# An expert stage written out for 64 experts, with thirteen weight places, narrower slot rows, and the last-slot weights transposed at the end

## The reference, cut to what matters

```
scores = softmax(h @ gate_weight.T)            # 2048 tokens x 64 experts
# 3 of 8 groups by their maximum, then the 6 best experts: topk_w, topk_i
pos  = running count of the expert over all (token, k)
slot = topk_i * 96 + minimum(pos, 95)          # later ones overwrite the last slot
buf  = zeros.at[slot].set(h[token])            # 64 x 96 x 256
out  = (silu(buf @ Wg.T) * (buf @ Wu.T)) @ Wd.T    # per expert, M = 176
y    = sum_k out[slot] * topk_w
shared = (silu(h @ Sg.T) * (h @ Su.T)) @ Sd.T  # 352 wide
x + gb * (y + shared)
```

## Time and profile before

| | |
|---|---|
| median of 3 runs | 1085.55 us (1081.42 to 1085.63) |
| profiled execution | 1088.81 us, its span 1087.0 us, mean granted clock 0.98 |
| busy: PE, DVE, ACT, POOL | 92%, 55%, 52%, 37% of the span |
| attention | to about 790 us |
| shared expert, last routing | about 790 to 857 us |
| expert stage, first to last scatter | 864.9 to 1053.6 us |
| the end | to 1087.0 us |

### The profile page before, as it was taken

One profiled execution on the slowest core, in us unless ns is written; L12 is line 12 of the kernel. 1 busy time (PEld: TensorE's weight loads), 2 busy tenths in 40 slices (PEclk: granted clock), 3 DMA queues, 4 the chain that ended last, 5 costly groups with the idle time before them and its releaser, 6 DMA issues.

```text
span 1087.0 us, 17987 instructions
## 1 busy us (share of the span) xinstructions
PE 1005.2 (92%) x6045; PEld 877.3 (81%) x6045; DVE 600.1 (55%) x1419; ACT 565.9 (52%) x1041; POOL 405.6 (37%) x598
## 2 busy tenths in 40 slices
PE   4999999999999999999999999999999888788883
PEld 4899999999999999999999999999755545444452
DVE  3555556666568656666865766685476311111117
ACT  2666666666766666676665666666430233233320
POOL 3122222233224554322455422255507244444450
PEclk9899999999999999999999999999999999999985
DMA  9990000001000110100011012000040499999946
GB/s 351 340 351 13 0 0 1 1 1 39 1 2 25 50 50 25 39 2 2 25 49 37 15 40 85 2 11 23 3 140 4 118 250 249 239 252 259 248 77 220
DMA packets 60138, 98.85 MB, mean 91 GB/s; under 512 B 8127, under 2 KB 41674, under 8 KB 59560
## 3 DMA queue, kind: packets, MB, share of 16 engines
q1 hardware_dynamic: 41992, 76.90, 21.6%
q0 software_dynamic: 11808, 14.16, 6.5%
q10 hardware_dynamic: 6272, 6.93, 2.4%
HBM read 65.31 MB, written 40.68 MB: 98 GB/s over the span
## 4 chain that ended last, share of the span: by engine, by line
PE 68%; DMA 14%; DVE 10%; issue 4%; ACT 2%; POOL 1%; POOLq 0%; SPq 0%; ACTq 0%; DVEq 0%
PE ps L1216 23%; DMA acc<-wos,arena 12%; PE ps L1266 12%; PE ps L1242 11%; PE ps L1255 9%; PE ps L1225 2%; PE ps L1228 2%; PE ps L1303 2%; PE ps L1249 2%; PE ps L1372 1%; PE ps L1426 1%; DMA arena<-slot_rows 1%; DVE ss L819 1%; DVE bst L746 1%; DMA warena<-in_wqkv 1%
## 5 line engine op out<-in xcount | busy, mean ns | idle before, releaser
L421 POOL TENSOR_TENSOR holdp<-neghalf 128x1 f32<-128x1 f32 x145 | 31.1, 215 | 477.2 <-ACT prob L583 242.0
L577 ACT ACTIVATE prob<-ps,rn 128x512 f32<-128x512 f32 (+3 forms) x256 | 121.0, 526 | 137.1 <-PE ps L1242 129.4
L1216 PE MATMUL ps<-wh,hth 128*128 128x384 f32 x512 | 178.2, 348 | 5.4 <-DVE htl L772 3.2
L1216 PE MATMUL ps<-wh,htl 128*128 128x384 f32 x512 | 172.9, 338 | 0.0
L1216 PE MATMUL ps<-wl,hth 128*128 128x384 f32 x512 | 172.7, 337 | 0.0
L819 DVE TENSOR_REDUCE ss<-arena 128x8 f32<-128x1024 f32 x64 | 78.1, 1220 | 150.6 <-ACT arena L553 150.5
L1266 PEld LDWEIGHTS ps<-vx,prob 128*128 128x128 f32 x1280 | 152.9, 191 | 3.9 <-POOL prob L468 0.7
L1266 PE MATMUL ps<-vx,prob 128*128 128x129 f32 (+1 forms) x1280 | 153.4, 274 | 0.4 <-POOL prob L468 0.4
L553 ACT ACTIVATE arena<-ps 128x1024 f32<-128x1024 f32 x64 | 65.5, 1023 | 141.3 <-PE ps L1216 141.3
L532 POOL DMA_INDIRECT acc<-wos,arena x64 | 90.2, 1409 | 116.8 <-DMA acc<-wos,arena 80.3
L1255 PE MATMUL ps<-wos,arena 128*128 128x256 f32 (+1 forms) x512 | 121.0, 379 | 0.8 <-ACT arena L587 0.8
(11 more groups left out here) (177 smaller groups left out, 1876.8 us busy)
## 6 DMA issues: line engine op xcount, KB each, us to landing
wge<-in_wgu SPq DMA_DIRECT2D x32, 352.0 KB, 4.5
slot_rows<-pay SPq DMA_DIRECT2D x1, 7728.0 KB, 37.4
arena<-slot_rows ACTq DMA_DIRECT2D x56, 120.8 KB, 4.1
wde<-in_wd SPq DMA_DIRECT2D x32, 192.0 KB, 4.2
prob<-in_wgu SPq DMA_DIRECT2D x16, 352.0 KB, 4.6
arena<-in_wgu SPq DMA_DIRECT2D x16, 352.0 KB, 4.2
warena<-in_wqkv SPq DMA_DIRECT2D x1, 4992.0 KB, 20.8
acc<-zrow SPq DMA_DIRECT2D x2, 2048.0 KB, 29.9
```

Of the source, the lines that this page charges most:

```text
L577: act_(prob[:, OFF[j]:OFF[j] + w], sflat[:, OFF[j]:OFF[j] + w], ACT.Tanh, scale=rn[:, bass.ds(head(n), 1), TT + j:TT + j + 1].squeeze(1)). ...
L1216: last = mm(ps[:, i, 0:3 * DH], hp[:, k, i * P:(i + 1) * P], wp[:, k, :], start=(k == 0 and m == 0), stop=(k == KC - 1 and m == 2))
```

## The change

It does these things:

- The ring of weights has 13 places. Seven gate/up places (GEARLY) and four down places are filled at the program's start, the other six and nine in the burst behind attention. Two accumulators stay.
- PE, ACT, DVE and SP have all 64 experts written out, with constants for addresses and waits.
- A slot row has 269 words: h, six weights, six expert numbers, the token. `route_probs` and its wait are gone; DVE multiplies the six best values by the inverse sum. For each expert DVE picks the weight with one compare-multiply-sum into `wcol`, and ACT takes its scale from there.
- The modulation's rows: `rcur` holds three rows of the current batch and is loaded anew for each batch by SP, `rgb` the gate row of all four.
- The transposes of w95 and their copies (now ACT's) come behind the last expert; w95's weights are formed with one more DVE operation per batch.
- At the end DVE multiplies the last rows by the gate rows of the batches (`o95g`), PE multiplies by that, and DVE adds PE's product to x as soon as it is there (`last_added`), and the accumulators' sum, scaled, later (`sums_added`).

```
-RING = 8
+GEARLY = 7
+RING = 13
-RW = 322
-TOK = D + E
+TOK = D + 2 * K
+RW = TOK + 1
...
-        rows = sb("rows", [P, B, 4, D])
+        rcur = sb("rcur", [P, 3, D])
+        rgb = sb("rgb", [P, B, D])
...
+            for u in range(GEARLY):
+                sp.dma_start(wgus[u], wgu[u]).then_inc(w_in[u], 16)
             for u in range(EARLY):
-                sp.dma_start(wgus[u], wgu[u]).then_inc(w_in[u], 16)
                 sp.dma_start(wds[u], wd[u]).then_inc(w_in[u], 16)
...
+            def rows_of(b):
+                sp.dma_start(rcur[:].rearrange("p c d -> p (c d)"),
+                             mod_d[b, 0:3, :].rearrange("c d -> (c d)").unsqueeze(0).to_broadcast([P, 3 * D])).then_inc(s["rows_in"], 16)
...
                 sp.dma_start(h2_rows[:, bass.ds(b, 1)].squeeze(1), pay[:, :, 0:D]).then_inc(s["h2_out"], 16)
+                rows_of(b + 1)
...
             for u in range(EARLY, RING):
-                sp.dma_start(wgus[u], wgu[u]).then_inc(w_in[u], 16)
+                if u >= GEARLY:
+                    sp.dma_start(wgus[u], wgu[u]).then_inc(w_in[u], 16)
                 sp.dma_start(wds[u], wd[u]).then_inc(w_in[u], 16)
...
+            for e in range(E + 2):
+                if e + RING < E:
+                    gate_up(e)
+                if e >= 2:
+                    if e - 2 + RING < E:
+                        down(e - 2)
+                    last_row(e - 2)
...
-            def route_probs(b):
-
-                a.wait_ge(s["sum_inv"], b + 1)
-                for i in range(TT):
-                    ins = act_(pay[:, i, D:TOK], lg[:, i, :], ACT.Copy, scale=rs[:, i:i + 1])
-                ins.then_inc(s["probs"], 1)
...
+                a.wait_ge(s["wcol_rdy"], base + e + 1)
                 act_(orow[:, e % ORING, :], ps[0:C, 4 + e % 2, 0:D], ACT.Copy,
-                     scale=xg[0:C, e % XR, bass.ds(D + (base + e), 1)]).then_inc(s["orow_rdy"], 1)
+                     scale=wcol[:, e % XR, 0:1]).then_inc(s["orow_rdy"], 1)
...
-            for e in range(XR):
-                e_period(e, 0)
-            with a.Fori(1, E // XR - 1) as r:
-                for e in range(XR):
-                    e_period(e, r * XR)
-            for e in range(E - XR, E):
+            for e in range(E):
                 e_period(e, 0)
             e_orow(E - 2, 0)
             e_orow(E - 1, 0)
+            for q in range(4):
+                a.wait_ge(s["w95_ps"], q + 1)
+                act_(w95t[:, q * T:(q + 1) * T], ps[0:E, (6 + q) % 8, :], ACT.Copy).then_inc(s["w95_sb"], 1)
...
                 v.wait_ge(s["y_added"], cnt(b, H - 1))
+                v.wait_ge(s["rows_in"], 16 * (b + 2))
...
-                step(b, cp(eif.rearrange("p (i k) -> p i k", i=TT), ei[:, :, 0:K]))
+                step(b, cp(pay[:, :, D + K:TOK], ei[:, :, 0:K]))
+                step(b, tt(pay[:, :, D:D + K], w8[:, :, 0:K], e3(rs, K), ALU.mult), False)
...
-                step(b, tt(w95[:, bass.ds(b * TT, TT), :], over, pay[:, :, D:TOK], ALU.mult))
+                step(b, tt(over, over, lg, ALU.mult))
+                step(b, tt(w95[:, bass.ds(b * TT, TT), :], over, e3(rs, E), ALU.mult))
...
-            for q in range(4):
-                v.wait_ge(s["w95_ps"], q + 1)
-                cp(w95t[:, q * T:(q + 1) * T], ps[0:E, 6 + q % 2, :]).then_inc(s["w95_sb"], 1)
...
+            def e_weight(e):
+                v.wait_ge(xg_in[e % XR], 16 * (e // XR + 1))
+                nc.vector.scalar_tensor_tensor(out=wcol[:, e % XR, 2:2 + K], in0=xg[0:C, e % XR, D + K:TOK], scalar=float(e),
+                                               in1=xg[0:C, e % XR, D:D + K], op0=ALU.is_equal, op1=ALU.mult,
+                                               accum_out=wcol[:, e % XR, 0:1]).then_inc(s["wcol_rdy"], 1)
...
+            v.wait_ge(s["o95_ld"], 16)
+            tt(o95g, o95.unsqueeze(1).to_broadcast([E, B, D]), rgb[0:E], ALU.mult).then_inc(s["o95_g"], 1)
+            last_added(0)
+            last_added(1)
+            sums_added(0)
+            last_added(2)
+            sums_added(1)
+            last_added(3)
+            sums_added(2)
+            sums_added(3)
...
-            for q in range(4):
-                if q >= 2:
-                    pe.wait_ge(s["w95_sb"], q - 1)
-                for i in range(TT):
-                    last = pe.transpose(ps[0:E, 6 + q % 2, i * P:(i + 1) * P], w95[:, q * TT + i, :], ident[:])
-                last.then_inc(s["w95_ps"], 1)
...
+            for q in range(4):
+                for i in range(TT):
+                    last = pe.transpose(ps[0:E, (6 + q) % 8, i * P:(i + 1) * P], w95[:, q * TT + i, :], ident[:])
+                last.then_inc(s["w95_ps"], 1)
+
+            pe.wait_ge(s["w95_sb"], 4)
+            pe.wait_ge(s["o95_g"], 1)
```

More of the change, by code:

```diff
@@ L205, in wd_place, with acc_of, adds @@
             return v.rearrange("p (m d) -> p m d", m=2)
-        wgus = [wge[:, u] for u in range(EARLY)]
-        wgus += [gu_place(prob[:, 0:2 * KC * M]), gu_place(prob[:, 2 * KC * M:4 * KC * M])]
-        wgus += [gu_place(arena2[:, late:late + 2 * KC * M]), gu_place(arena2[:, late + 2 * KC * M:late + 4 * KC * M])]
+        GW, DW, tail = 2 * KC * M, 2 * D, half + 4096
+        wgus = [wge[:, u] for u in range(GEARLY)]
+        wgus += [gu_place(prob[:, u * GW:(u + 1) * GW]) for u in range(2)]
+        wgus += [gu_place(arena2[:, late + u * GW:late + (u + 1) * GW]) for u in range(2)]
+        wgus += [gu_place(warena[:, tail + u * GW:tail + (u + 1) * GW]) for u in range(2)]
         wds = [wde[:, u] for u in range(EARLY)]
-        wds += [wd_place(vx[0:MR, 1024:1536]), wd_place(vx[0:MR, 1536:2048]), wos[0:MR, 4:6, :], wos[0:MR, 6:8, :]]
+        wds += [wd_place(vx[0:MR, (u + 1) * DW:(u + 2) * DW]) for u in range(3)]
+        wds += [wos[0:MR, c:c + 2, :] for c in (4, 6, 11, 13)]
+        wds += [wd_place(arena2[0:MR, late + 2 * GW:late + 2 * GW + DW]), wd_place(warena[0:MR, tail + 2 * GW:tail + 2 * GW + DW])]
+        assert late + 2 * GW + DW <= 4096 and len(wgus) == RING and len(wds) == RING
         accs = [warena[:, a * NT * D:(a + 1) * NT * D].rearrange("p (i d) -> p i d", i=NT) for a in range(NACC)]
+        def acc_of(e):
+            return e % NACC
+        def adds(a, e):
+            return 16 * sum(acc_of(n) == a for n in range(e))
         tri = sb("tri", [P, P])
@@ L369, in _, with gate_up, down, last_row @@
                 sp.dma_start(xg[0:C, e, :], buf_d[e * C:(e + 1) * C, :]).then_inc(xg_in[e], 16)
[L371 to L401, removed]
+            def gate_up(e):
+                sp.wait_ge(s["gu_ps"], e + 1)
+                sp.dma_start(wgus[e % RING], wgu[e + RING]).then_inc(w_in[e % RING], 16)
+            def down(e):
+                sp.wait_ge(s["dn_ps"], e + 1)
+                sp.dma_start(wds[e % RING], wd[e + RING]).then_inc(w_in[e % RING], 16)
+            def last_row(e):
+                sp.wait_ge(s["orow_rdy"], e + 1)
+                sp.dma_start(o95_d[e:e + 1], orow[C - 1:C, e % ORING, :]).then_inc(o95s[e % ORING], 16)
+            for e in range(E + 2):
[5 more added lines that the diff above has]
+                    last_row(e - 2)
             for u in range(ORING):
@@ L1434, in tr2, with down @@
                 last.then_inc(s["tr2_ps"], 1)
-            def down(e, base):
-                pe.wait_ge(s["actt_rdy"], base + e + 1)
-                if not (isinstance(base, int) and base + e < 2):
-                    pe.wait_ge(s["orow_rdy"], base + e - 1)
+            def down(e):
+                pe.wait_ge(s["actt_rdy"], e + 1)
+                if e >= 2:
+                    pe.wait_ge(s["orow_rdy"], e - 1)
                 for m in range(2):
@@ L1472, in _ @@
                     t = b * TT + i
[L1473 removed]
+                    last = mm(ps[:, 2 * b + i // 2, (i % 2) * D:(i % 2 + 1) * D], w95t[:, t * P:(t + 1) * P], o95g[:, b, :], start=True, stop=True)
                 last.then_inc(s["cmb_ps"], 1)
```

164 lines of the change are left out of this document (73 added, 91 removed).

## The result

The changed kernel takes **1075.52 us** (median of 7 runs, 1073.38 to 1078.1), the kernel before 1085.55 beside it: ratio 0.9913, 95% interval 0.9894 to 0.9932. It is faster, by 10.0 us. Forecast were 1074.0 us, range 1068 to 1083. The profiled execution took 1077.3 us, span 1075.5: 11.5 less than the one before, against a forecast of 11.4.

The account below looks back on a forecast made before the run. TensorE is 92% busy overall, but DMA work and the scatter chain, taken as one story, slow the expert stage's middle. -2.6 - 3.7 - 3.8 - 1.3 = -11.4 us: 1077.4 profiled, 1074 median, range 1068 to 1083.

Parts of the forecast that it names:

- Start, -2.6: Start of expert stage: w95's transposes leave the shared stage, first row transposes at 854.4 instead of 857.05, 2.6 us saved.
- Thirteen places, -3.7: Expert stage: last weight load triggered by expert 50, not 55, so five more experts run at 2.37, not 3.10; 3.7 us saved.
- Narrow rows, -3.8: Middle of expert stage: slot row of 269 instead of 322 words saves 0.077 us for each of 49 experts, 3.8 us.
- if the middle is bound by DMA work, 49 experts gain it: Condition of the narrow-rows term in the expert stage: 0.077 us per expert, 3.8 us in all; lower bound 0.
- Rival A: Middle of expert stage: scatter latency, not DMA work, sets the pace; narrow rows give nothing, -7.6, 1078 us; chance 0.20.
- Loops written out, 0: Expert stage: ACT's loop edges cost 2.7 us but under a wait for a landing; counted 0, -2.7 kept for the range.
- The new DVE operation, 0: Expert stage: a 96x6 operation with a sum per expert, 0.23 each, some 15 us in all, covered, so 0.
- The end, -1.3: Closing part: DVE has 14 operations left instead of 16 and ends at 1082.4 against 1083.7, 1.3 us saved.
- if PE keeps 2.4 GHz through its transposes: Closing products: at that clock the batches take half the time and the end gives -2.3 instead of -1.3.

Follow-up runs that it names:

- the halved weights: Changed kernel, but expert-stage reloads of gate/up weights bring only the first half of each tile (other half stale); 1072.08 us, ratio 0.9827 to the kernel before.
- eight places, wide rows: Changed kernel with the weight ring back at 8 places and the slot row padded from 269 to 322 words again; 1081.70 us, ratio 0.9973.
- index copied: Changed kernel with DVE copying each expert's token index into its own ring, so row loads no longer wait for the scatter; 1083.21 us, ratio 0.9970.
- row 95 on ACT's queue: Index copied, plus the 1 KB copy of row 95 issued by ACT instead of SyncE and 40 idle transposes before the closing products; 1072.37 us, ratio 0.9893.

## Why the prediction was right, and where it was not

**Start, -2.6: right.** 854.38 and 854.4 was the estimate; the releaser is DVE's L1079, and the row loads landed under it. The experiment that undoes the move puts the start 3.9 us back and costs 2.2 us by ratio, which with an uncertainty of 2.4 agrees with 2.6 and doesn't prove it.

**Thirteen places, -3.7: right in kind, the size only bounded.** 2.8 us on the mean of nine traces, 2.4 between the two stages, 5.8 by ratios (uncertainty 2.7). The mechanism is in the windows: the DMA share falls to 0.82 from 1000 us and to 0.50 from 1020, while before it was 0.95 on the mean up to 1036. From expert 49 on scatters are 2.31 apart, against 2.54 for the same experts before.

**Narrow rows, -3.8: too high.** 0.8 us by ratios (uncertainty 2.3), some 1.1 by the slope of the halved weights. The step that failed is "if the middle is bound by DMA work, 49 experts gain it", and the reason given for the full value, that q10's time goes by bytes. It does: q10 went from 2.4% to 2.0%. But the stage's time does not go by q10's. Rival A named what sets the pace, the scatter's latency, and put this part at nothing, which the ratios allow too. The pair of traces at the top, whose middle shows just the forecast 3.8, is luck: two traces of the changed kernel differ by 1.7 there.

**What does set the pace.** The prediction saw the chain of two accumulators, but costed it at (5.1 + 0.75) / 2 = 2.93, below the 3.10 of the middle, and so put the rest down to DMA work and took both as one story. The 0.75 for the issue was too small. A scatter starts 0.85 us at the least behind the landing of the one two before. The means of experts 4 to 49, worked out from the semaphores' updates in the traces:

| | scatter lands in | next on the chain starts behind that | half the sum | pace |
|---|---|---|---|---|
| kernel before | 5.19 | 1.04 | 3.12 | 3.12 |
| eight places, wide rows | 5.12 | 1.01 | 3.07 | 3.08 |
| changed kernel | 5.04 | 1.01 | 3.03 | 3.05 |
| index copied | 5.47 | 0.97 | 3.22 | 3.25 |
| row 95 on ACT's queue | 4.98 | 0.96 | 2.97 | 3.00 |

That half the sum is the pace is arithmetic. That the chain binds is shown by 33 to 38 of 46 scatters in each of these kernels starting within 0.95 us of that landing, near the least there is. The work of the DMA engines acts through the landing, 3.3 us at best and 5 under load. A third accumulator takes 0.12 to 0.15 us per expert off, and then the engines stand at a share of 1.01; a quarter less bytes takes 0.19 to 0.22 off with the chain kept. Neither alone reaches PE's 2.39, and what both together would give wasn't run. 20 KB less on the row load's queue is too little to be told from scatter (4.9 us in the median with either width). Freeing the row loads from the scatter gives nothing by itself; the pace with it is 3.00 once row 95 is out of SyncE's queue, and 3.01 in the second trace of the changed kernel.

**Loops written out, 0: right**, ratio 1.0005. The Trainium skill, Runtime: NRT & Kernel Launch, Instruction fetch mechanics, says that kernels prefer full unrolling where possible; it brings no gain here, and the 0.45 us of ACT's edge lay under a wait. **The new DVE operation, 0: right.** It takes 0.15 + 0.08 us, as its nearest row said.

```profile
903.90 0.15 DVE L1136 SCALAR_TENSOR_TENSOR arena<-arena 96x6 f32<-96x6 f32 x1
903.98 0.08 DVE L1136 DVE_READ_ACCUMULATOR arena<-arena 96x1 f32 x1
```

**The end, -1.3: -1.7, right.** Counted from the last scatter, the products were said to start at +2.9 us (1055.3 + 1.2 less 1053.57) and start at +3.1; DVE's sums were said to start at +11.3 and start at +11.5. The 14 operations then take 16.96 us, 1.21 each and not 1.25, which makes up the 0.4 us. The kernel before with its loops written out, whose end is the same, has 32.10 us instead of 33.43, so that a figure of one trace is good to about 1 us.

```profile
1045.54 1.22 DVE L1178 TENSOR_TENSOR pay<-vx,rgb 64x1024 f32<-64x1024 f32 x1 [5.62 <-DMA vx<-last_rows]
...
1055.20 1.22 DVE L1166 TENSOR_TENSOR warena<-warena 128x1024 f32<-128x1024 f32 x1
...
1070.94 1.22 DVE L1171 TENSOR_TENSOR xs<-xs,warena 128x1024 f32<-128x1024 f32 x1
```

The last operation starts 27.2 us behind the last scatter, before it was 28.9. The condition "if PE keeps 2.4 GHz through its transposes" wasn't met: PE stood idle for 4.04 us behind them, for the last rows and the multiply by the gate rows. Where it was made to hold, the end was 29.23 us, 4.2 less than before, and not 2.3 as the forecast had for that case; DVE's sums then began 8.9 us behind the last scatter instead of 11.5, held only by the accumulators' loads (0.92 us).

So the total was right in part by luck. Narrow rows were some 3 us too high. What filled the gap isn't known part by part: the places by ratios may have given up to 2 us more than said, the end 0.4 more, and the rest is within the scatter of single executions (the changed kernel's two traces have stages of 181.64 and 179.94).

## What to carry to other kernels

A DMA share of 0.95 says that the engines are full and not that time goes by their bytes: look for who waits for a landing and how many places or chains share it, then take bytes and chain away separately, each beside an unchanged kernel of the same group. In a queue that waits for one thing after another, a small copy that needs a late result holds back the large loads behind it; give it another queue. Before believing or rejecting a releaser, count which write belongs to which scatter: the one that follows in time can be two experts off. Before a last block of products, see how long PE has been idle.

## What the runs showed of the hardware

- The 16 closing products (x32 in the trace) take 13.99 us at the granted clock 0.50 behind a pause of 4.04 us, 13.63 behind 2.06, and 7.14 behind 0.67.
- A POOL sum of 128x1024 float32 takes 2.72 us, and two DVE operations of the same size beside it 3.25 each instead of 1.22.
- A 1 KB copy behind weight loads of 352 and 192 KB on SyncE's queue lands in 1.1 to 4.1 us, though those loads themselves land 4.1 to 4.5 us from their issue. Where it had to wait for a late write, the load behind it was issued up to 4.0 us behind the product that freed its place.
- An indirect scatter starts at least 0.85 us behind the landing of the scatter it waits for.
- Eight more instruction packets cost nothing that can be measured.
